# Two steps of scores moved ahead of the second embedding, later packing of the third group's pixels, output weights split in halves, slot clearing behind the pixels

## What is computed

```
h = tok(x)                                   # patches @ W + b, class token, positions
h = concat([h, txt], axis=1)                 # [32, 114, 256]
h = h + attn(layernorm(h))                   # x + softmax(q k / 8 + causal) v @ Wo
h = h + ffn(layernorm(h))                    # top 2 of 8 experts, capacity 570, exact gelu

# attention, per head
scores = einsum('bqhd,bkhd->bhqk', q / sqrt(64), k) + where(causal, 0, -inf)
attn   = softmax(scores)
out    = einsum('bhqk,bkhd->bqhd', attn, v).reshape(B, S, 1024)
return x + out @ Wo
```

## Time and profile before

| | |
|---|---|
| time, median of 3 runs | 888.19 us (887.49 to 890.09) |
| profiled execution | 886.87 us |
| its span | 884.9 us |
| mean granted TensorE clock | 0.981 of full speed |
| PE busy | 829.8 us (94%) |
| DVE / ACT / POOL busy | 565.8 / 510.6 / 377.7 us |

### The profile page before, as it was taken

How to read it: one execution, slowest core, us unless ns; L and a number is a source line. 1 busy time by engine, 2 the same in 40 slices (tenths; PEclk the granted TensorE clock), 3 DMA queues, 4 the chain that set the end, 5 groups by cost and what they waited for, 6 DMA issues and landing times.

```text
span 884.9 us, 20230 instructions
## 1 busy us (share of the span) xinstructions
PE 829.8 (94%) x7019; PEld 752.6 (85%) x7019; DVE 565.8 (64%) x2477; ACT 510.6 (58%) x1717; POOL 377.7 (43%) x683
## 2 busy tenths in 40 slices
PE   4869999999999999999999999999569999999996
PEld 4758898888889888888888988988469999999995
DVE  3557537665774865766577486477557877668771
ACT  3567665764774666576477377566055655556551
POOL 3144343443643735554364373465614223441334
PEclk9979999999999999999999999999889999999998
DMA  7695569909635681990910100010446445553322
GB/s 233 90 110 143 162 66 87 76 23 91 93 30 73 90 70 31 110 91 21 100 30 1 41 28 6 10 32 3 122 128 194 110 129 115 128 136 92 70 28 28
DMA packets 99615, 71.22 MB, mean 80 GB/s; under 512 B 71453, under 2 KB 92123, under 8 KB 99400
## 3 DMA queue, kind: packets, MB, share of 16 engines
q1 hardware_dynamic: 80169, 59.04, 39.6%
q0 software_dynamic: 19072, 9.83, 7.1%
q10 hardware_dynamic: 272, 1.05, 0.3%
HBM read 50.88 MB, written 21.89 MB: 82 GB/s over the span
## 4 chain that ended last, share of the span: by engine, by line
PE 72%; DVE 11%; issue 6%; POOL 4%; DMA 4%; ACT 2%; SPq 1%; POOLq 0%; DVEq 0%
PE bank L422 13%; PE bank L423 12%; PE bank L424 12%; PE o_bank L1479 5%; PE score_bank L1459 4%; PE pT_bank L1468 4%; DVE sm L1134 2%; PE o_bank L423 2%; PE o_bank L424 2%; PE o_bank L422 2%; PE bank L1309 2%; PE score_bank L423 2%; PE score_bank L422 2%; PE score_bank L424 2%; POOL slots_dram L587 2%
## 5 line engine op out<-in xcount | busy, mean ns | idle before, releaser
L639 POOL TENSOR_SCALAR pr<-pr,rc 114x114 f32<-114x114 f32 x512 | 181.1, 370 | 289.6 <-DVE rc L1176 288.5
L813 ACT ACTIVATE pr<-sm,nb 114x114 f32<-114x114 f32 x512 | 192.3, 383 | 8.0 <-DVE nb L1138 7.9
L670 POOL DMA_INDIRECT out_dram<-yout,dest x40 | 74.1, 1851 | 159.5 <-ACT yout L861 153.2
L1134 DVE CUSTOM_DVE_ANT_0 sm<-score_bank,mask 114x114 f32<-114x114 f32 x512 | 109.9, 272 | 47.8 <-PE score_bank L1459 47.7
L786 ACT ACTIVATE oT_hi<-o_bank 128x228 fp32r<-128x228 f32 x128 | 45.4, 355 | 125.1 <-PE o_bank L1479 89.7
L422 PE MATMUL bank<-xT_hi,wqkv_hi 128*128 128x456 f32 (+1 forms) x288 | 111.2, 386 | 1.4 <-DVE qk L891 1.4
L807 ACT ACTIVATE pT<-pT_bank 114x456 f32<-114x456 f32 x128 | 70.6, 552 | 54.7 <-PE pT_bank L1468 54.3
L423 PE MATMUL bank<-xT_lo,wqkv_hi 128*128 128x456 f32 (+1 forms) x288 | 101.1, 351 | 0.0
L424 PE MATMUL bank<-xT_hi,wqkv_lo 128*128 128x456 f32 (+1 forms) x288 | 100.3, 348 | 0.0
L813 ACT ACTIVATION_READ_ACCUMULATOR pr<-sm,nb 114x1 f32 x512 | 99.0, 193 | 0.0
L1468 PE MATMUL pT_bank<-ident,pr 114*114 114x114 f32 x512 | 75.1, 269 | 0.7 <-ACT pT L807 0.7
(11 more groups left out here) (224 smaller groups left out, 2236.2 us busy)
## 6 DMA issues: line engine op xcount, KB each, us to landing
stage_a<-in_L_ffn_w_dram SPq DMA_DIRECT2D x8, 1024.0 KB
stage_b<-in_L_ffn_w_dram SPq DMA_DIRECT2D x8, 1024.0 KB
slots_dram<-fill SPq DMA_DIRECT2D x8, 605.6 KB
xs<-slots_dram SPq DMA_DIRECT2D x8, 363.4 KB
pix<-in_x_dram SPq DMA_DIRECT2D x12, 216.0 KB
pix<-in_x_dram SPq DMA_DIRECT2D x12, 211.5 KB
pix<-in_x_dram SPq DMA_DIRECT2D x12, 207.0 KB
out_dram<-h SPq DMA_DIRECT2D x8, 308.0 KB
```

Source lines behind the costliest of these rows:

```text
L639: p = pool.tensor_scalar(pr[:, m % 4, i, :], pr[:, m % 4, i, :], rc[:, m % 4, i:i + 1], 1.0, ALU.mult, ALU.mult)
L670: pool.indirect_dma_start(out, bass.IndirectOffsetOnAxis(ap=dest[e % 2][:, t:t + 1], axis=0), yout[:, t, :], None, compute_op=ALU.add).the ...
L813: a = act.activation(pr[:, N % 4, i, :], sm[:, N % 2, i, :], ACT.Exp, bias=nb[:, N % 2, i:i + 1], scale=SCALE, accum_out=rs[:, N % 4, i:i ...
L1134: m = dve.tensor_tensor_reduce(sm[:, N % 2, i, :], score_bank[i % 2][0:T, o:o + T], mask[:, :], 1.0, NEG, ALU.add, ALU.max, mx[:, N % 2, i ...
```

## The change

The scores of steps 0 and 1 are computed right after Q0 and the pixel transposes of group 1, ahead of K1 and of `embed_first(1)`. For this `first_W` moves to a place in memory where it does not overlap the tiles `sm` and `pr`. The second half of the Q weights is split (ACT) after the exponentials of step 0, and on DVE at the start of step 1; the drain of group 1's embedding goes with it. The turning of the first expert bias (job B) moves from ahead of step 0 into step 2. The first half of group 2's pixels is packed in step 4, no longer in step 2. The output weight is split in two halves, in steps 2 and 3 on ACT and 3 and 4 on DVE. SP waits for both halves of group 2's pixels before it issues the clearing of the slots.

```diff
-        first_W = nc.alloc_sbuf_tensor_at("first_W", [128, JS, D], F32, offset=used[0] + 4 * KC * JS * 128)
         sm = place("sm", [T, 2, 4, T])
         pr = place("pr", [T, 4, 4, T])
+        first_W = nc.alloc_sbuf_tensor_at("first_W", [128, JS, D], F32, offset=used[0])
+        first_W_end = used[0] + 4 * JS * D
...
-        AT_PACK, AT_RSTD1, AT_RSTD2 = [(2, 11)] + [(5, 11)] * (G - 1), 10, 8
+        AT_PACK, AT_RSTD1, AT_RSTD2 = [(4, 11)] + [(5, 11)] * (G - 1), 10, 8
         AT_WO = 2
+        AT_B = 2
...
+            if (g, n) == (0, AT_B):
+                jobs.append(("B", 0, "d"))
...
-                + [("V", 2 * b, "a") for b in range(1, GB)] + [("K", 0, "a"), ("Q", 0, "d"), ("K", 1, "a"), ("P0", 2, "a"), ("P0", 3, "a"), ("M", 1, "d"), ("B", 0, "d")])
-        PROLOGUE = len(JOBS)
+                + [("V", 2 * b, "a") for b in range(1, GB)] + [("K", 0, "a"), ("Q", 0, "d"), ("P0", 2, "a"), ("P0", 3, "a"), ("K", 1, "a"), ("M", 1, "d")])
...
             def clear_slots():
+                sp.wait_ge(pix_in, 16 * SH * packed_units(2, 1))
                 sp.wait_ge(fill_done, 2)
...
             pack_first(1, 1)
-            drain_k(1)
             drain_patches(1, 0)
             drain_patches(1, 1)
-            split_columns(0, 1, stage_b, wq_in, wq_hi)
+            drain_k(1)
...
-                if N == AT_WO:
-                    split_high(wo_hi[:, :, :], stage_d[:, :].rearrange("p (c n) -> p c n", c=HP), wo_in, wo_hi_done)
+                if N - AT_WO in range(2):
+                    split_high(*wo_half(wo_hi, N - AT_WO), wo_in, wo_hi_done)
+                if N == 0:
+                    split_columns(0, 1, stage_b, wq_in, wq_hi)
...
             split_columns(2 * HD, 1, stage_a, wv_hi, wv_lo)
-            drain_embedded(1)
-            split_columns(0, 1, stage_b, wq_hi, wq_lo)
-            drain("B", 0, b1T[:, :], job_bank("B", 0)[:, 0:E * MC])
...
+                if N == 1:
+                    drain_embedded(1)
+                    split_columns(0, 1, stage_b, wq_hi, wq_lo)
+                if N == AT_B + 1:
+                    drain("B", 0, b1T[:, :], job_bank("B", 0)[:, 0:E * MC])
...
             project("K", 0)
             project("Q", 0)
+            transpose_first(1)
+            for N in range(2):
+                scores(N)
             project("K", 1)
-            transpose_first(1)
             embed_first(1)
-            pe.wait_ge(b1_in, 16)
-            dst = claim("B", 0)
-            pe.transpose(dst[:, 0:E * MC], b1_raw[:, :], ident[0:E * MC, 0:E * MC]).then_inc(filled, 1)
             pe.wait_ge(consts_done, CONSTS)
```

More of the change, by code:

```diff
@@ L173, in build @@
         attention_end = used[0]
-        used[0] = oT_at
+        used[0] = first_W_end
         tok_raw = place("tok_raw", [128, KC, CH * PX * PX])
@@ L434, in turned_weights, with wo_half @@
                     tok_raw[:, dc, :].rearrange("p (c r h j) -> p c j h r", c=CH, h=SH, j=JJ))
+        def wo_half(dst, i):
+            c = slice(i * HP // 2, (i + 1) * HP // 2)
+            return dst[:, c, :], stage_d[:, :].rearrange("p (c n) -> p c n", c=HP)[:, c, :]
         def first_patches(g, h):
@@ L779, in take_outputs @@
                 if m == 0:
-                    act.wait_ge(filled, PROLOGUE)
+                    act.wait_ge(filled, job_filled("B", 0))
                     act.wait_ge(wk_lo, 2)
-                    act.wait_ge(wo_lo_done, 1)
+                    act.wait_ge(wo_lo_done, 2)
                 elif f > 0 and c == 0:
@@ L1195, in _ @@
                     route(g - 2, ROUTE_NEXT[n])
-                if N == AT_WO + 1:
-                    dve.wait_ge(wo_hi_done, 1)
-                    split_low(wo_lo[:, :, :], stage_d[:, :].rearrange("p (c n) -> p c n", c=HP), wo_hi[:, :, :], wo_lo_done)
+                if N - AT_WO - 1 in range(2):
+                    dve.wait_ge(wo_hi_done, N - AT_WO)
+                    whole = wo_half(wo_lo, N - AT_WO - 1)
+                    split_low(*whole, wo_half(wo_hi, N - AT_WO - 1)[0], wo_lo_done)
                 if N == STEPS + 2:
@@ L1406, in project_o @@
                 if g == 0:
-                    pe.wait_ge(wo_lo_done, 1)
+                    pe.wait_ge(wo_lo_done, 2)
                 pe.wait_ge(o_lo, PAIRS * g + PAIRS - 1 + i)
@@ L1509, in _ @@
             project("Q", 0)
+            transpose_first(1)
+            for N in range(2):
+                scores(N)
             project("K", 1)
-            transpose_first(1)
             embed_first(1)
-            pe.wait_ge(b1_in, 16)
-            dst = claim("B", 0)
-            pe.transpose(dst[:, 0:E * MC], b1_raw[:, :], ident[0:E * MC, 0:E * MC]).then_inc(filled, 1)
             pe.wait_ge(consts_done, CONSTS)
-            pe.wait_ge(small_in, SMALL)
             for N, g, n in steps():
@@ L1524, in _ @@
                     for m in (N, N + 1):
-                        if m < STEPS:
+                        if 1 < m < STEPS:
                             scores(m)
@@ L1531, in _ @@
                     transpose_probs(N - LAG_T)
+                if N == AT_B:
+                    pe.wait_ge(b1_in, 16)
+                    dst = claim("B", 0)
+                    pe.transpose(dst[:, 0:E * MC], b1_raw[:, :], ident[0:E * MC, 0:E * MC]).then_inc(filled, 1)
+                    pe.wait_ge(small_in, SMALL)
                 if g < G:
```

## The result

The changed kernel takes **879.99 us** (median of 4 runs, 878.66 to 880.83) against 888.66 (4 runs, 887.49 to 890.09): a ratio of 0.9897, 95% interval 0.9881 to 0.9913. That is 8.7 us less; 878.4 was predicted. The profiled execution took 878.66, its span is 876.7 against 884.9: 8.2 us less.

What follows compares the result with a forecast made beforehand. PE, busy 94% of the span, was taken as the bound, so only its idle and slow stretches could be won. 10.9 us removed less 1.1 gave 9.8: 888.2 - 9.8 = 878.4 us, 8-in-10 range 876.0 to 882.5.

Steps and rivals of the forecast that it cites:

- The stall and what stood around it: Pixel transposes to step 6 scores: stall 5.55, half clock 2.6, embedding wait 1.27, Q-drain waits 1.5; 10.9 us removed.
- the predicted sum: Whole change: 10.9 us removed less the 1.1 us new wait, a gain of 9.8 us.
- stall and half clock: PE's 5.55 us idle before the first `pT`, and 2.6 us lost in the following work at clock 0.50.
- The new wait in step 5: PE wants to overwrite `pT_bank` at 50.9 but ACT's second `pT` copy ends at 52.0: 1.1 us.
- The port: Step 2's bias and POOL's `hx` compete for the shared port; bias expected at 45.5, `hx` at about 45.6.
- the rival: The bias loses the port to `hx` and waits 1.2 us: gain 8.6, time 879.6 us; chance 0.2.
- The packing of step 4: Pixels land by 52.65, 0.85 us before ACT packs them at 53.5; up to 2.7 us later would cost nothing.
- The clearing and step 21: Clearing and everything behind come about 1.3 us later; pixels (3,0) in by about 125, ACT waits up to 5 us.
- the price of 0: ACT's wait at step 21 priced at 0 for PE, with ends 0 and 3; K drain 2.1 us in time.
- My edge of 127.1: Step 21: pixels (3,0) landed later than 127.1 make PE wait, each further microsecond being one of PE.
- the stall moves to step 21: Rival: pixels (3,0) land late behind the clearing and PE catches up; time 879 to 883 us; chance 0.1.

Runs made afterwards that it cites:

- the packing alone: The kernel before, with only the packing of the first half of group 2's pixels moved from step 2 to step 4: 880.74 us, ratio 0.9906.
- the two kernels show in which ACT is out of the way: The changed kernel with the output weight split whole (880.26 us), and with its second half split in step 4 on ACT, step 5 on DVE (878.99 us).
- the second profile of the changed kernel: The changed kernel run and profiled again with no edit: 881.59 us, ratio 0.991.
- the kernel with `hx` late: The changed kernel with the output weight's second half split in steps 4 and 5 and POOL's group 0 `hx` additions moved there: 883.42 us, ratio 0.9941.
- the two clearings more: The changed kernel with ten blocks cleared in place of eight, the additional two in memory nobody reads: 889.14 us, ratio 0.9998.
- the version with the clearing behind: The changed kernel with the clearing of the slots issued behind pixels (3,0): 877.8 us, ratio 0.9861; again 878.09 us, ratio 0.9871.
- both late `hx` versions with a wrong queue order: The changed kernel with late second half and `hx`: 883.42 us; the same with clearing behind pixels (3,0) and pixels (2,1) ahead of the text: 885.29 us.

## Why the prediction was right

**The stall and what stood around it: right, to a tenth.** 29.26 + 1.23 (K1 has moved in) - 20.67 = 9.8 us, the predicted sum. The parts: the number for the packing alone takes 6.7 of it; the rest, 3.1, comes with the order of the scores and the halves, of which the halves are 0.87. I had 8.15 for stall and half clock (5.55 + 2.6). The half clock can be read off: the same instructions of PE, from the weighing to the scores of step 6, take 7.95 us before (57.05 to 65.00) and 5.55 after without the new wait (49.88 to 56.43, less 1.00), so it cost 2.4, not 2.6. The packing alone gives less than that, since a new wait for `pT` of 1.2 us takes a part's place in the old order. No clock below 1.00 stands between 30 and 75 us.

**The new wait in step 5: right in size (1.0 against 1.1), only half right in cause.** ACT's chain was followed well: with the 1.25 us of the later start taken off, the first `pT` is done at 48.6 (48.65 predicted), the second at 51.9 (52.0). But POOL's `pr` is late by nearly as much, as the two kernels show in which ACT is out of the way. I had not followed POOL through step 5.

**The port: the rival did not come at the bias, but the collision came elsewhere.** The bias stood 0.16 us ahead of `hx` and took 0.21 us. DVE's low half of the output weight, which I had laid where DVE waits for scores anyway, is the step hit: the first half of the low part took 2.33 us beside the second `hx` (1.26, it began 0.06 us earlier) where it takes 1.26 alone, and POOL's eight `pr` operations took 4.72 in place of about 2.8 (an estimate, twice the 1.40 for four of the earlier trace rows). The Trainium skill states in "SBUF — State Buffer", section "Who interferes with whom", that a DVE instruction with two SBUF inputs contends with a GpSimd instruction that reads SBUF, and that the shared ports are an exclusive lock. The trace agrees in its times: `hx` ended at 50.63 and DVE's split 1.13 us later, and POOL's eight operations took 1.9 us more than alone. It hid behind the wait for `pT`.

**The packing of step 4: no cost, as said, with a smaller margin.** The pixels came 18.55 us after their issue began (36.80 to 55.35), not 17.15; ACT waited 0.72 us, and PE did not.

**The clearing and step 21: the price of 0 was right, the margin was not.** I had pixels (3,0) in by 125 and up to 5 us of ACT's wait; they came at 128.49 and ACT waited 7.20. 1.25 of the 3.5 us come from the later start. The term that was mis-sized is the wait ahead of the clearing. I had it put everything behind it 1.3 us later, a number that no row gave. The kernel without it has the pixels at 123.13 with the transposes at 34.53; with it they come at 128.49 with the transposes at 35.76, so it costs 4.1 (5.1 by the second profile of the changed kernel). Part of this is the time that pixels (2,1) take: the clearing began 17.8 us after their issue, and I had read 16.2 (54.79 to 71) from the transfers' share, which doesn't show when the last of a group is in. My edge of 127.1, moved by 1.25, is 128.35, and the pixels landed 0.14 behind it with no wait of PE; the same kernel's other profile has 8.1 us of wait and 0.86 of PE. So the rival "the stall moves to step 21" is the one that was nearest to coming true, with up to 0.9 us. Its mechanism, the edge and one for one behind it, is shown by the kernel with `hx` late and by the two clearings more.

**From 9.8 to 8.2.** The transposes started 1.25 us later than predicted: the low clock from 26 to 30. The way from the transposes of `tok_turned` to these is 14.70 us after (21.06 to 35.76). In the version with the clearing behind it is 13.54, at clock 1.00 throughout:

```profile
20.48 0.65 PE L1502 MATMUL bank<-ident,tok_turned 128*128 128x128 f32 x4 [1.27 <-DVE hraw L973]
...
34.02 1.02 PE L1332 MATMUL bank<-ident,first_pix 72*128 72x72 f32 x12
```

So the low clock costs 1.2 us. It stands in 5 of the 14 profiles of this study, one of them with the old order of the scores, and not in the changed kernel's second one: no part of the change. That it fell into the profile of the result is luck; the last section has another such difference, at the start of the program. 0.1 us went in the steps after 6, and 0.2 behind the last scores. The median came 1.6 us above the forecast: these, and a kernel before that was 0.5 slower in this comparison than the 888.19 from which I had counted.

## What to carry to other kernels

When a transfer ends a wait, move the work that needs it and not the work around it: one number in a table gave about two thirds of this gain in the profile (6.7 of 9.8 us) and, by the medians, a ratio (0.9906) that can't be told from the whole change's, while all the rest without it gave 0.3%. Then follow each queue that is now asked sooner to its next customer, and count the microseconds to the point where the wait reaches the bounding engine; here a later step had 7.2 us of cover, and an added wait had used it up unseen. A microsecond saved on one engine by delaying another's work is lost many times over if a transfer is queued behind that work: both late `hx` versions with a wrong queue order were slower than without it.

## What the runs showed of the hardware

- The granted clock can be 0.50 for some 3 us while PE is busy throughout, in some executions of a kernel and not in others: between 25 and 31 us in 5 of 14 profiles (about 1.2 us lost), and from 526 to 534 on in 4 of 14, 1.6 us lost in three of them and 3.2 in the one where it lasted 7 us, over a third of the gain of the change. One profile has it at 375 us and one at 230, 0.8 to 1.1 us each.
- Waits of PE of 3.65, 4.78, 5.55, 7.72 and 9.32 us were each followed by 4.7 to 6.1 us at clock 0.50; those of 1.0 to 1.3 us in the stretch by none.
- DVE's two-operand split of 128x1024 values and POOL's work hold each other up: 2.33 against 1.26 us on DVE, 4.72 against some 2.8 us for eight operations on POOL.
- A stall that the profile puts down to "issue" can be a wait for a semaphore whose other side is itself waiting: 4.78 us of PE were DVE's 6.6 us for the text.
- The transposes of `tok_turned` that the lines above show stand at 20.48 to 21.17 us in eleven profiles and at 22.28, 22.97 and 23.30 in three, in kernels that agree up to there. In these three the embedding ahead of them (24 matmuls, begun at 12.85 to 13.34) took 4.92, 6.10 and 6.10 us in place of 3.18, with matmuls of 0.45 us in place of 0.29: PE was not yet at its full clock. (The profile's clock records begin only at 16.9 to 19.2 us there, and its tables say 1.00 ahead of them; the length of the matmuls tells.) One of the three is the changed kernel's second profile. So one span against another tells no better than 3 us; a stretch counted from an instruction behind it tells tenths.
